# Turning attention probabilities with VectorE squares and a trip through memory instead of TensorE transposes

## The reference, cut to what matters

```
Q = xpos(X @ W_Q);  K = xpos(X @ W_K, downscale=True);  V = X @ W_V
p = softmax(Q @ K^T, axis=-1) * D          # D[n, m] = 0.9 ** |n - m|, 1024 x 1024
x = layernorm(X + p @ V)
gate = fp4_linear(x, w_gate); y = fp4_linear(x, w_up)     # 256 -> 704
x = layernorm(x + fp4_linear(silu(gate) * y, w_down))     # 704 -> 256
```

## Time and profile before

| what | value |
|---|---|
| median of three runs | 1030.32 us |
| span of the profiled execution, first to last instruction | 1028.9 us |
| TensorE matmuls busy | 98% of the span |
| VectorE busy | 87% |
| GpSimd busy | 73% |
| ScalarE busy | 57% |
| granted TensorE clock | full (2.4 GHz) in all slices |
| moved by DMA | 47.23 MB |

### The profile page before, as it was taken

How to read it: one execution, slowest core, us unless ns; L and a number is a source line. 1 busy time by engine, 2 the same in 40 slices (tenths; PEclk the granted TensorE clock), 3 DMA queues, 4 the chain that set the end, 5 groups by cost and what they waited for, 6 DMA issues and landing times.

```text
span 1028.9 us, 20101 instructions
## 1 busy us (share of the span) xinstructions
PE 1009.9 (98%) x6490; PEld 917.9 (89%) x6490; DVE 894.9 (87%) x1876; ACT 582.5 (57%) x1451; POOL 752.7 (73%) x973
## 2 busy tenths in 40 slices
PE   8899999999999999999999999999999999999996
PEld 7788999999999999999999999999999999989885
DVE  7989988888888889898888988889888888988886
ACT  3655556655665655655565665566556565565543
POOL 5977868776786867778687686876768686776654
PEclk9999999999999999999999999999999999999999
DMA  8020111110120101201020010211112020000000
GB/s 304 11 68 7 62 41 54 42 62 12 42 82 12 62 22 33 82 21 58 16 83 32 22 62 17 78 42 25 49 41 79 15 63 17 17 21 22 21 11 26
DMA packets 28263, 47.23 MB, mean 46 GB/s; under 512 B 2816, under 2 KB 21504, under 8 KB 26240
## 3 DMA queue, kind: packets, MB, share of 16 engines
q1 hardware_dynamic: 27472, 44.90, 13.8%
q10 hardware_dynamic: 688, 1.05, 0.3%
HBM read 37.55 MB, written 8.39 MB: 45 GB/s over the span
## 4 chain that ended last, share of the span: by engine, by line
PE 85%; POOL 5%; DVE 5%; issue 4%; DMA 1%; ACT 0%; SPq 0%; POOLq 0%; DVEq 0%; ACTq 0%
PE ps_g L491 11%; PE ps_g L492 11%; PE ps_g L493 11%; PE ps_oy L491 9%; PE ps_oy L493 9%; PE ps_oy L492 9%; PE ps_t L500 9%; PE ps_s L491 5%; PE ps_s L492 5%; PE ps_s L493 5%; POOL h L2019 2%; PE ps_oy L500 1%; DMA first_gate_up<-w_up 1%; PE ps_oy L677 1%; PE ps_oy L676 1%
## 5 line engine op out<-in xcount | busy, mean ns | idle before, releaser
L2019 POOL TENSOR_TENSOR h<-h,hsc 128x704 f32<-128x704 f32 x252 | 202.4, 815 | 58.8 <-DVE h L1511 28.5
L2116 POOL TENSOR_TENSOR prob<-prob,decay_t 128x512 f32<-128x512 f32 x128 | 163.6, 1292 | 4.0 <-ACT prob L1058 3.6
L491 PE MATMUL ps_oy<-v_h,pt_h 128*128 128x256 f32 x512 | 150.5, 294 | 0.0
L491 PE MATMUL ps_g<-wgu_h,xqt_h 128*128 128x480 f32 (+1 forms) x380 | 149.6, 394 | 0.4 <-DVE xqt_l L1548 0.3
L493 PE MATMUL ps_oy<-v_h,pt_l 128*128 128x256 f32 x512 | 144.8, 283 | 0.0
L492 PE MATMUL ps_oy<-v_l,pt_h 128*128 128x256 f32 x512 | 144.8, 283 | 0.0
L493 PE MATMUL ps_g<-wgu_h,xqt_l 128*128 128x480 f32 (+1 forms) x380 | 142.6, 375 | 0.0
L492 PE MATMUL ps_g<-wgu_l,xqt_h 128*128 128x480 f32 (+1 forms) x380 | 142.6, 375 | 0.0
L491 PE MATMUL ps_s<-k_h,q_h 128*128 128x512 f32 x256 | 104.8, 409 | 0.0
L491 PEld LDWEIGHTS ps_oy<-v_h,pt_h 128*128 128x128 f32 x512 | 97.7, 191 | 3.3 <-DVE pt_l L1529 1.7
L492 PE MATMUL ps_s<-k_l,q_h 128*128 128x512 f32 x256 | 100.6, 393 | 0.0
(11 more groups left out here) (260 smaller groups left out, 3053.7 us busy)
## 6 DMA issues: line engine op xcount, KB each, us to landing
rope_t<-rope SPq DMA_DIRECT2D x15, 1024.0 KB, 5.3
xres<-x SPq DMA_DIRECT2D x64, 128.0 KB, 2.0
out<-yout SPq DMA_DIRECT2D x63, 128.0 KB, 1.7
xin<-x_t SPq DMA_DIRECT2D x14, 512.0 KB, 4.1
first_rope<-rope SPq DMA_DIRECT2D x2, 512.0 KB, 8.4
decay_t<-decay SPq DMA_DIRECT2D x1, 960.0 KB, 12.2
first_down<-w_down SPq DMA_DIRECT2D x1, 704.0 KB, 10.3
first_gate_up<-w_gate SPq DMA_DIRECT2D x2, 256.0 KB, 7.8
```

Of the source, the lines that this page charges most:

```text
L491: pe.matmul(dst, a_h, b_h, start=(start and i == 0), stop=False)
L2019: return tt(blocks(dst), blocks(src), sc[:, which, at:at + n].unsqueeze(2).to_broadcast([P, n, QB]), ALU.mult)
L2116: tt(prob[:, keys], prob[:, keys], decay_t[:, lo:lo + CW], ALU.mult).then_inc(decayed, 1)
```

## The change

Tiles 2 to 62 "cross". For them VectorE's transpose turns `prob` half by half inside squares of 32 x 32 into `turned`, ordered so that the four blocks of 32 columns that belong to one block of partitions lie together. SyncE stores each half (256 KB) to an internal DRAM tensor `parking`, waits for its arrival, and loads it with four DMAs (64 KB each, in pieces of 512 bytes) into `landing`, each to 32 partitions. ScalarE's `landed_high` copies each half from `landing` to `pt_h`. For half 0 GpSimd subtracts (`landed_low`) from `landing`; for half 1 ScalarE also copies `landing` to the PSUM bank `ps_t[:, 1]` (`landed_copied`), and VectorE subtracts from there. Tiles 0, 1 and 63 keep the TensorE transposes; tile 63's go to `ps_s`.

The values product now belongs to tile s - 2, gate_up to s - 3, h to s - 4, down to s - 5 and the store to s - 6 (`LAG` 6). `first_norm` moves from VectorE to ScalarE, as scale and shift, and GpSimd's `r1_shift` makes the shift. `h_copied` is gone: `h_quantised` writes 640 columns, and then the last 64 twice into a buffer `h_last` of its own. tanh, gated and silu of parts 1 and 2 move from the next step into the step of their gate_up. The lists of all engines are new. Cut to its core (the lists of the split and plain steps stand for those of the others):

```diff
@@ constants @@
-LAG = 5
+LAG = 6
...
+FIRST_CROSSING, LAST_CROSSING = 2, LAST_TILE - 1
+QUADS = 4
+QUAD = P // QUADS
@@ SyncE @@
+parking = nc.dram_tensor("parking", [2, 2, P, CW], F32, kind="Internal").ap()
...
+def park(i, g):
+    if crosses(i):
+        sp.wait_ge(turned_done[g], crossing(i))
+        wait(sp, landed[g], 16 * QUADS * (crossing(i) - 2))
+        sp.dma_start(parking[i % 2, g], turned[:, g, :]).then_inc(parked[g], 16)
+def land(i, g):
+    if crosses(i):
+        sp.wait_ge(parked[g], 16 * crossing(i))
+        sp.wait_ge(ptl_done[g], i)
+        if g == 1:
+            sp.wait_ge(pth_done[1], i)
+        rows = parking[i % 2, g].rearrange("(a j) (c x) -> c j a x", a=QUADS, c=QUADS)
+        for c in (0, 2, 1, 3):
+            sp.dma_start(landing[c * QUAD:(c + 1) * QUAD, g, :].rearrange("p (a x) -> p a x", a=QUADS),
+                         rows[c]).then_inc(landed[g], 16)
@@ SyncE, rotation step @@
+if s % NT in (0, 2, 4, 6):
+    park(one, 0)
+    store(six)
+    land(one, 0)
+    park(one, 1)
+    load_x(s)
+    load_residual(one)
@@ SyncE, split step @@
+park(one, 0)
+store(six)
+park(one, 1)
+land(one, 0)
+load_rope(s)
+land(one, 1)
+load_residual(one)
@@ TensorE, split step @@
-prob_transposes(prev, 0)
+values_product_first(two)
+down(five)
 scores(now, 0)
-prob_transposes(prev, 1)
+values_product_second(two)
+x1_transposes(three)
 scores(now, 1)
-x1_transposes(gu)
-values_product_first(prev)
-values_product_second(prev)
-gate_up(gu, 0)
-down(fin)
-gate_up(gu, 1)
-h_transposes(dn, 0)
-h_transposes(dn, 1)
-gate_up(gu, 2)
+projected()
+gate_up(three, 0)
+gate_up(three, 1)
+h_transposes(four, 0)
+h_transposes(four, 1)
+gate_up(three, 2)
@@ ScalarE @@
+def landed_high(i, g):
+    if crosses(i):
+        act.wait_ge(landed[g], 16 * QUADS * crossing(i))
+        wait(act, (o_first_done, o_done)[g], i)
+        nc.scalar.copy(keys_by_quad(pt_h[:, half_of_keys(g), :]), landed_half(g)).then_inc(pth_done[g], 1)
+def landed_copied(i):
+    if crosses(i):
+        act.wait_ge(landed[1], 16 * QUADS * crossing(i))
+        wait(act, ptl_done[1], i)
+        wait(act, htl_done, 2 * (i - 3) + 2)
+        nc.scalar.copy(keys_by_quad(ps_t[:, 1]), landed_half(1)).then_inc(copied, 1)
...
-wait(act, pt_done, 2 * i)
+if crosses(i - 1):
+    for g in range(2):
+        act.wait_ge(turned_done[g], crossing(i - 1))
+else:
+    wait(act, pt_done, 2 * i)
...
+def first_norm(i):
+    if live(i):
+        wait(act, nb1_done, i + 1)
+        wait(act, r2_done, i - 3)
+        nc.scalar.activation(x1[:, i % 4, :], r1, ACT.Identity, bias=nb1[:, 0:1],
+                             scale=rs1[:, 0:1]).then_inc(x1_done, 1)
@@ ScalarE, split step @@
+output(six)
+landed_copied(two)
+landed_high(two, 1)
+new_x_high(c_x)
+x_magnitude(three)
+h_magnitude(four)
+r2_mean(five)
+x1_high(three)
+r2_squares(five)
+rotated_high(*turned)
+r1_mean(two)
+tanh(three, 0)
+r1_squares(two)
 exponential(now)
-h_high(dn, 0)
-h_high(dn, 1)
+h_high(four, 0)
+h_high(four, 1)
+tanh(three, 1)
+tanh(three, 2)
+landed_high(one, 0)
+first_norm(two)
@@ VectorE @@
+def turn(i, g):
+    if crosses(i):
+        dve.wait_ge(decayed, 2 * i + g + 1)
+        wait(dve, parked[g], 16 * (crossing(i) - 1))
+        nc.vector.transpose(turned[:, g, :].rearrange("p (c n q) -> p n c q", c=QUADS, n=NT // 2),
+                            prob[:, g * CW:(g + 1) * CW]).then_inc(turned_done[g], 1)
+def landed_low(i):
+    if crosses(i):
+        dve.wait_ge(copied, crossing(i))
+        dve.wait_ge(pth_done[1], i + 1)
+        wait(dve, o_done, i)
+        keys = half_of_keys(1)
+        tt(pt_l[:, keys, :], ps_t[:, 1], pt_h[:, keys, :].bitcast(F32), ALU.subtract)\
+            .then_inc(ptl_done[1], 1)
@@ VectorE, rotation step @@
+x_scales(three)
+row_inverse(two)
+turn(one, 0)
+h_max(four)
+x_reciprocals(three)
+h_scales(four)
+landed_low(two)
+h_reciprocals(four)
+second_residual(five)
+turn(one, 1)
+x_shift(three)
 rot_mul(*rot, 0)
+x_grid(three)
+h_shift(four)
 rot_mul(*rot, 1)
+xqt_low(three)
+h_grid(four)
+first_residual(two)
 row_max(now)
+gated(three, 0)
+silu(three, 0)
+h_low(four, 0)
+h_low(four, 1)
+gated(three, 1)
+x_max(two)
+gated(three, 2)
+silu(three, 1)
+silu(three, 2)
@@ GpSimd @@
+def doubled(src, sc):
+    twice = [P, 2, LAST // QB, QB]
+    return tt(h_last[:].rearrange("p (u n k) -> p u n k", u=2, k=QB),
+              blocks(src).unsqueeze(1).to_broadcast(twice),
+              sc.unsqueeze(1).unsqueeze(3).to_broadcast(twice), ALU.mult)
...
+whole = F - LAST
+if g == 0:
+    hv = h[:, i % 2, 0:whole]
+    times_scale(hv, hv, hsc, 0).then_inc(hq_done, 1)
+else:
+    wait(pool, ht_done, 2 * i)
+    doubled(h[:, i % 2, whole:], hsc[:, 0, whole // QB:]).then_inc(hq_done, 1)
...
+def r1_shift(i):
+    if live(i):
+        wait(pool, rs1_done, i + 1)
+        tt(nb1[:], nm1[:], rs1[:], ALU.mult).then_inc(nb1_done, 1)
...
+def landed_low(i):
+    if crosses(i):
+        pool.wait_ge(pth_done[0], i + 1)
+        wait(pool, o_first_done, i)
+        keys = half_of_keys(0)
+        tt(keys_by_quad(pt_l[:, keys, :]), landed_half(0), keys_by_quad(pt_h[:, keys, :]).bitcast(F32),
+           ALU.subtract).then_inc(ptl_done[0], 1)
@@ GpSimd, split step @@
+x_units(three)
+h_units(four)
+x_quantised(three)
+new_x_low(c_x)
+h_quantised(four, 0)
+r2_variance(five)
+r2_inverse(five)
+h_quantised(four, 1)
+r1_variance(two)
+r1_inverse(two)
+rotated_low(*turned)
+r1_shift(two)
+r2_shift(five)
 decay_half(now, 0)
 decay_half(now, 1)
+landed_low(one)
```

More of the change, by code:

```diff
@@ L1173, in _ @@
             probs_high(1, 1)
-            x_magnitude(0)
             exponential(2)
-            x1_high(0)
-            tanh(0, 0)
-            r1_mean(1)
-            r1_squares(1)
+            first_norm(0)
             def step(s):
-                now, prev, gu, dn, fin, end = (s - lag for lag in range(6))
+                now, one, two, three, four, five, six = (s - lag for lag in range(7))
                 rot, turned, c_v, c_x = rotation(s), rotation(s - 1), values_chunk(s), split_chunk(s)
@@ L1728, in _ @@
             probs_low(1, 1)
-            x_shift(0)
-            x_grid(0)
             rot_mul(1, 2, 0)
             rot_mul(1, 2, 1)
-            xqt_low(0)
-            first_residual(1)
-            gated(0, 0)
-            silu(0, 0)
-            first_norm(1)
-            x_max(1)
-            x_scales(1)
-            x_reciprocals(1)
+            x_max(0)
             def step(s):
-                now, prev, gu, dn, fin = (s - lag for lag in range(5))
+                now, one, two, three, four, five, six = (s - lag for lag in range(7))
@@ L2169, in _ @@
             r1_inverse(0)
+            r1_shift(0)
             new_x_low(2)
-            x_units(0)
             rotated_low(0, 1)
-            x_quantised(0)
             decay_half(2, 0)
             decay_half(2, 1)
-            r1_variance(1)
-            r1_inverse(1)
-            x_units(1)
             rotate(1, 2, 0)
             def step(s):
-                now, prev, gu, dn, fin, end = (s - lag for lag in range(6))
-                rot, turned, c_v, c_x = rotation(s), rotation(s - 1), values_chunk(s), split_chunk(s)
+                now, one, two, three, four, five, six = (s - lag for lag in range(7))
+                rot, turned, c_x = rotation(s), rotation(s - 1), split_chunk(s)
@@ L2293, in _ @@
             r2_shift(last - 4)
-            h_copied(last - 2)
+            h_quantised(last - 3, 0)
+            h_quantised(last - 3, 1)
+            r1_variance(last - 1)
+            r1_inverse(last - 1)
+            r1_shift(last - 1)
+            x_units(last - 1)
+            last_inverse(0)
+            h_units(last - 2)
+            x_quantised(last - 1)
+            x_units(last)
+            r2_variance(last - 3)
+            r2_inverse(last - 3)
+            r2_shift(last - 3)
             h_quantised(last - 2, 0)
```

983 lines of the change are left out of this document (491 added, 492 removed).

## The result

Before took 1030.32 us (1030.21 to 1030.91), the changed kernel 1102.61 (1101.78 to 1102.92): a ratio of 1.0698 [1.0678, 1.0717]. I had forecast 993 and given 9 in 100 to slower. The profiled execution's span is 1101.0 us beside 1028.9.

What follows compares the result with a forecast made beforehand. TensorE was taken as the bound, its work being the time: 1030.3 - 53.1 + 2 (last batch) + 8 (pairs) + 4 (ends) + 2 (last tiles' transposes in idle time) = 993 us, range 985 to 1005 at chance 0.50.

Steps and rivals of the forecast that it cites:

- TensorE's 53.1 us: Tiles 2 to 62 lose eight TensorE transposes of 0.87 us in all each, 61 x 0.87 = 53.1 us saved.
- The turn, 0.6 us: VectorE's transpose of 128x512 was taken at 0.6 us, the pace of a plain subtraction, two a tile.
- rival (c): VectorE's turn takes 1.21 us, making the kernel slower than before, 1061 us; decided from a turn of 1.0 us; chance 0.06.
- The 1.24 us: VectorE's turn of 512 columns if it took four times the skill page's 311 ns for a 128x128 bf16 transpose.
- The trip through memory at nothing: SyncE's stores and loads of the turned halves, a round trip of 5.5 to 6 us, were costed at nothing.
- Rival (d): The halves land late, 2 us a tile for 61 tiles: 1099 us at worst; chance of slower 0.03.
- The last batch, +2 us: VectorE's 12.7 to 13.2 us against TensorE's 12.6 in plain steps: 0.3 us late in each of 7, 2 us.
- Pairs of steps, +8 us: GpSimd falls behind in tiles 1 and 5 of a batch: 0.55 us a pair, 14 pairs in 7 batches, 8 us.
- signs of being right: TensorE's waits, if any, at x1 transposes or the values product's second half, around tiles 1 and 5.
- Ends, +4 us: Start and drain: one more stage moves a tile's work from start to end, 4 us lost, bounds 0 and 8.
- The sign: Whole kernel: faster by over 0.2% had chance 0.88, within it 0.03, slower 0.09.

Runs made afterwards that it cites:

- e5: Changed kernel with scores and down ahead of values_product_first in TensorE's split, plain and last steps, plus four reordered items in the drain: 1068.22 us.
- e8: e5 without the trip through memory, with turns, landed_low, landed_high and landed_copied on 32 of 512 columns: 1012.2 us.
- e3: Changed kernel without the ten DMAs a tile to parking and landing; landing filled once, ScalarE's copies wait for the turn: 1103.91 us.
- e1: Changed kernel with TensorE's scores and down ahead of values_product_first in the split, plain and last steps: 1079.43 us.
- e7: e5 without the trip through memory, whole turns, GpSimd's landed_low of the lower keys on 32 of 512 columns: a middle batch 3.6 us shorter.
- e6: e5 without the trip through memory, each VectorE turn on 32 of 512 columns: a middle batch 3.0 us shorter.
- e17: e5 with h_scales of every tile up to the 59th made by ScalarE instead of VectorE: 1069.24 us.
- e12: e5 without ScalarE's landed_copied; VectorE's landed_low of the upper keys reads the landing tile in SBUF: 1108.99 us.
- e4: Changed kernel with only the drain reordered: SyncE's store of tile 58 and GpSimd's x_quantised(62) and h_quantised(62) go earlier: 1091.84 us.
- e14: e5 with GpSimd's new_x_low and rotated_low in the split step moved behind r1_shift and r2_shift, ahead of the decays: 1096.22 us.

## Why the prediction was wrong, step by step

**The size of the miss.** The kernel took 110 us more than forecast: some 48 in the six middle batches, 33 in the last batch, and nearly 30 in the drain. No one term gave the sign; e5, with the loop and the drain's orders mended, is still slower than before.

**TensorE's 53.1 us.** Nearly right as work: with the new operations nearly free (e8) a batch takes 118.2, where 115.9 were forecast, and TensorE waits for 0.6 us of it. In the changed kernel the saving does not come as time, since TensorE stops being the bound.

**The turn, 0.6 us.** A record of 0.70, and 0.63 to the next start, as forecast; rival (c) needed 1.0. The 1.24 us that the prediction also priced did not come. Not the cause.

**The trip through memory at nothing.** Right (e3). Rival (d), late halves, has the nearest time (1099), but not the mechanism: in the whole run ScalarE stands for the landing four times, for 3.0 us. The data land in time, the work on them is late. That the nearest number stood beside a wrong mechanism is chance.

**The last batch, +2 us.** This step failed. I summed VectorE's work in a plain step (11.7 plus 1.0 to 1.5) and set it against TensorE's 12.6, as if a step were as long as its fullest queue. The prediction nowhere follows landed_low(one) to its reader. In the step with a rotation values_product_first is TensorE's fourth item; in the split, plain and last steps it is the first, and the producer is GpSimd's last. Both meet only where such steps follow each other, in the last batch; a split step is followed by one with a rotation. That is why e1 left the middle batches as they were. Most of the steps took 17.6 us, and the batch 33 us more than the forecast of some 91. The order of two items gave back 23 (e1); landed_low's work alone another 8.0 (e7 beside e5); e8 is at 90.5, where the forecast had it.

**Pairs of steps, +8 us.** This step failed by the most: 8 us for the seven batches, where it became 7.9 us for each of the six in the middle (124.9 beside 117). The places and the work were right. GpSimd's list in the split step, 16.1 us in the sum, runs without a break from 530.43 to 546.54 in e5, and the step takes 16.6. The waits are the two that I had named as signs of being right, x1_transposes for GpSimd's xv and the values product for pt_l. The size was wrong: I let TensorE's buffers and the next step take back all but 0.55 us of a pair, with 1.6 as the upper bound. In the changed kernel TensorE stands for 1.15 us for landed_low at the head of a split step and for 1.02 for x_quantised behind it, 2.2 us a pair, and for 1.5 more in other steps of the batch. So the buffers took back little. By e6 to e8, 6.8 us of the 9.1 over the forecast of TensorE's work hang on the time of the new operations, some 3 on each queue. The other 2.3 stay when they are nearly free; only 0.6 of them is a wait that the profile shows, and what the rest is stays open. Where VectorE's work comes off or on matters as much as how much: 9.9 us off gave 3.0 us (e6), 4.4 us of another kind nothing (e17), and 4.1 us more cost 4.6 (e12).

**Ends, +4 us.** +30.5 (35.0 in the drain, -4.5 in front). This step failed too, and its own sign of being wrong, a drain longer by over 8 us, came. I took the stage more as work that moves from one end to the other. From the last exponential on the trace has 282 matmuls beside before's 230, and little other work is there to cover their waits: TensorE is busy for 47 of 78.6 us. 11.2 us were bad order (e4). The other 23 or so remain with the new operations nearly free (66.8 in e8). So they come with the longer pipeline or with the orders of the drain that are left; no run tells these two apart.

**The sign.** A sum over the busiest queue can't show a loop. One glance at each kind of step, for every new operation, asking who is late behind it and where the reader stands, would have shown GpSimd's last item feeding TensorE's first. That is worth 23 us here; for the rest, VectorE's and GpSimd's waits for one another had to be added up along the chain, step by step.

## What to carry to other kernels

When a change adds a stage handed from engine to engine, place producer and consumer in every kind of step list, not in the commonest: last in one list and first in the next makes a loop whose period is the sum of its parts. Before moving an operation out of a full queue, look for the wait that it fills (e14); before moving one, in or off, make it nearly free and time that, which costs one run and bounds the gain (e8 said that with these lists at most 18 us were to be had). A deeper pipeline is paid at the drain, where nothing covers it.

## What the runs showed of the hardware

- VectorE's small SBUF to SBUF scaling (128x44) takes 0.14 us at best and up to 1.13, and each of the 24 instances over 0.45 ended 40 to 49 ns behind the end of a GpSimd instruction; the profile shows the wait as the instruction's own duration. A subtraction of 128x512 with both inputs in SBUF takes 0.67 to 1.85 us, with one in PSUM 0.67 to 0.69.
- VectorE's transposition in 32x32 squares, 128x512 in f32: 0.70 us, the pace of a plain subtraction, and never stretched beside GpSimd (0.65 to 0.71 over 122).
- 1 MB a tile of stores and loads, 110 GB/s instead of 43 in a middle batch, left every engine's busy time within 0.3 us (e3).
- TensorE's matmuls of 256 columns had a pitch of 0.21 instead of 0.12 us behind a wait of 3.3 us, at a granted clock of 0.55 (956.84 to 960.60).
